# Rotary embedding in a decoder kernel: the sine products and sums of the rotation move from GpSimd to VectorE

## The reference

```
def apply_rope(t, freqs):
    rot = freqs.shape[-1]                       # 32 of the 64 features of a head
    t1, tp = (t[..., :rot], t[..., rot:])
    rh = jnp.concatenate([-t1[..., d2:], t1[..., :d2]], axis=-1)
    t1 = t1 * jnp.cos(freqs) + rh * jnp.sin(freqs)
    return jnp.concatenate([t1, tp], axis=-1)
...
q = q * DH ** (-0.5); q = apply_rope(q, pe_q); k = apply_rope(k, pe_k)
sim = jnp.einsum('bhid,bhjd->bhij', q, k)       # 8 heads of 64
a = jax.nn.softmax(sim, axis=-1)                # self-attention: masked first
out = jnp.einsum('bhij,bhjd->bhid', a, v)
```

## Time and profile before

| | |
|---|---|
| median of 3 runs | 4260.31 us (4253.38 to 4267.61) |
| profiled execution | 4263.09 us, its span 4261.1 us |
| busy | PE 3944.9 us (93%), DVE 2716.7 (64%), ACT 2011.2 (47%), POOL 986.7 (23%) |
| mean granted TensorE clock | 0.976 of full speed |

### The profile page before, as it was taken

The page is one execution under the profiler, slowest core; times in us unless marked ns, Lnnn a source line. Parts: engine busy times, 40 slices in busy tenths (PEclk is TensorE's granted clock), DMA queues, the critical chain, the costliest instruction groups (busy, mean ns, idle before and its releaser), DMA issues. The chain is left out here.

```text
span 4261.1 us, 70671 instructions
## 1 busy us (share of the span) xinstructions
PE 3944.9 (93%) x23644; PEld 2415.2 (57%) x23644; DVE 2716.7 (64%) x7580; ACT 2011.2 (47%) x5804; POOL 986.7 (23%) x1068
## 2 busy tenths in 40 slices
PE   7898899999999999999988988999999999999998
PEld 4644445565655655666646444455555556555665
DVE  4576667777777645764445776677777776456644
ACT  2633445555555534663226234456555555346632
POOL 2144423333222200000020443232333221000000
PEclk9899999999999999999988999999999999999999
DMA  2000000000000010010010000000000000100000
GB/s 91 6 17 1 1 23 17 23 17 23 17 23 2 25 57 21 14 53 9 8 54 5 17 1 1 23 17 23 17 23 17 23 2 25 71 7 34 33 9 10
DMA packets 15849, 91.84 MB, mean 22 GB/s; under 512 B 2176, under 2 KB 8064, under 8 KB 12032
## 3 DMA queue, kind: packets, MB, share of 16 engines
q1 hardware_dynamic: 15488, 87.27, 5.7%
HBM read 86.22 MB, written 1.05 MB: 20 GB/s over the span
## 5 line engine op out<-in xcount | busy, mean ns | idle before, releaser
L606 PE MATMUL ps_O<-wide,V 128*64 128x256 f32 (+4 forms) x5152 | 597.1, 395 | 1.9 <-ACT wide L634 1.8
L559 PE MATMUL ps_S<-KT,QT 64*128 64x154 f32 (+7 forms) x1936 | 383.4, 463 | 59.1 <-POOL QT L1614 25.4
L652 POOL COPY RX<-recips 128x256 f32<-128x256 f32 (+2 forms) x356 | 156.5, 440 | 1195.7 <-DVE recips L730 1184.8
L741 DVE TENSOR_TENSOR QT<-ps_O,RS 128x512 f32<-128x512 f32 x212 | 146.6, 692 | 413.9 <-PE ps_O L606 410.8
L687 ACT ACTIVATE EX<-NB,neg 128x154 f32<-128x154 f32 (+3 forms) x640 | 349.8, 551 | 103.7 <-DVE neg L715 103.7
L606 PEld LDWEIGHTS ps_O<-wide,V 128*64 128x64 f32 (+4 forms) x5152 | 266.9, 128 | 195.6 <-issue 112.0
L636 DVE COPY wide<-ps_P 128x512 f32<-128x512 f32 (+4 forms) x484 | 311.0, 645 | 80.8 <-PE ps_P L588 79.3
L429 POOL TENSOR_TENSOR small<-small 128x4 f32<-128x4 f32 x112 | 113.6, 1014 | 1042.8 <-DVE small L414 879.2
L634 ACT ACTIVATE wide<-ps_P 128x512 f32<-128x512 f32 (+4 forms) x488 | 274.9, 564 | 149.2 <-PE ps_P L588 149.1
L559 PE MATMUL ps_T<-KT,QT 64*128 64x154 f32 (+5 forms) x968 | 325.8, 439 | 17.1 <-ACT EX L687 9.0
L559 PE MATMUL ps_OUT<-KT,QT 64*128 64x154 f32 (+5 forms) x968 | 335.8, 442 | 0.9 <-ACT EX L687 0.4
(11 more groups left out here) (379 smaller groups left out, 8404.2 us busy)
## 6 DMA issues: line engine op xcount, KB each, us to landing
weights<-in_w_dram SPq DMA_DIRECT2D x10, 1664.0 KB, 6.8
weights<-in_w_dram SPq DMA_DIRECT2D x2, 6148.0 KB, 17.4
weights<-in_w5next_dram SPq DMA_DIRECT2D x6, 1664.0 KB, 6.8
weights<-in_w_dram SPq DMA_DIRECT2D x2, 4200.0 KB, 13.0
weights<-in_reltab_dram SPq DMA_DIRECT2D x2, 4096.0 KB, 13.6
weights<-in_w_dram SPq DMA_DIRECT2D x8, 640.0 KB, 3.9
weights<-in_w_dram SPq DMA_DIRECT2D x5, 832.0 KB, 4.4
weights<-in_w_dram SPq DMA_DIRECT2D x2, 2050.0 KB, 8.0
```

Of the source, the lines that this page charges most:

```text
L559: ins = pe.matmul(S4[k][:, a * N:(a + 1) * N], QT[strip, c, qts[a] * P:(qts[a] + 1) * P], self.keys(c)[strip, 0:N], start=True, stop=True)
L606: ins = pe.matmul(O1[self.slot * j:self.slot * (j + 1), q0 * P:(q0 + self.nq) * P], self.value(c * self.hpc + j, kc), self.probs(rd, j)[:, ...
L652: pool.tensor_copy(RX[:, q0 * P:(q0 + self.nq) * P].rearrange("p (n s) -> p n s", s=self.slot), of.unsqueeze(2).broadcast_to([P, self.nq * ...
L741: dve.tensor_tensor(self.out_chunk(c), O1[:, :], RS[:, c % 2, :], ALU.mult).then_inc(r.av_sb, 1)
```

## The change

DVE does the whole rotation: every product by the sines and every sum. POOL keeps the powers and the spreads, and issues both powers at the start of the step. The sum on DVE waits for the cosine product and the sine product of its own rope. The semaphores and their counts stay as they were; `rotated` is now raised by DVE.

```
@@ rope @@
-            if sin is not None:
-                dve.wait_ge(r.evac_dve, 2 * j + 1)
-                dve.tensor_tensor(part, part, sin, ALU.mult).then_inc(r.sum_step, 1)
+            dve.wait_ge(r.evac_dve, 2 * j + 1)
+            dve.tensor_tensor(part, part, sin, ALU.mult).then_inc(r.sum_step, 1)
+            dve.wait_ge(r.evac_dve, 2 * j + 2)
+            dve.wait_ge(r.sum_step, j + 1)
+            dve.tensor_tensor(dst, dst, part, ALU.add).then_inc(r.rotated, 1)
@@ Attention.pool @@
-            def pool(self, pool, r, late=None):
-                for i in range(1, self.rounds + 1):
-                    for j in self.late.get(i - 1, ()):
-                        if j != "X":
-                            late(pool, j)
-                    self.spread(pool, r, i - 1)
+            def pool(self, pool, r):
+                for rd in range(self.rounds):
+                    self.spread(pool, r, rd)
@@ L1Attention @@
             def turning(self, j):
                 return (self.part(j), 0.125 if self.order[j][0] == "q" else None, self.before(j), j,
-                        self.sines(j) if self.cross or j < 2 else None)
+                        self.sines(j))
-            def rotate(self, pool, j):
-                r, d, part = self.r, self.dest(j), self.part(j)
-                pool.wait_ge(r.evac_dve, 2 * j + 2)
-                if not self.cross and j >= 2:
-                    pool.tensor_tensor(part, part, self.sines(j), ALU.mult).then_inc(r.sum_step, 1)
-                pool.wait_ge(r.sum_step, j + 1)
-                pool.tensor_tensor(d, d, part, ALU.add).then_inc(r.rotated, 1)
             def pool(self, pool):
                 self.fresh(pool)
-                self.rotate(pool, 0)
-                self.rotate(pool, 1)
-                self.prev.pool_tail(pool)
-                if self.prev.tail_parts == 1:
-                    self.nxt.pool_head(pool)
-                self.rotate(pool, 2)
-                self.rotate(pool, 3)
-                if self.prev.tail_parts > 1:
-                    self.nxt.pool_head(pool)
-                self.att.pool(pool, self.r, self.rotate)
+                self.pool_beside(pool)
+                self.att.pool(pool, self.r)
```

## The result

| | before | after |
|---|---|---|
| median | 4258.98 us (4 runs, 4253.38 to 4267.61) | 4428.28 us (4 runs, 4420.55 to 4435.48) |
| profiled execution, its span | 4263.09 us, 4261.1 us | 4420.55 us, 4419.0 us |
| mean granted clock | 0.976 | 0.958 |
| 14 self steps, mean and all | 65.42, 915.9 us | 71.61, 1002.5 us |
| the first self step of each pass | 72.76, 72.75 us | 74.21, 75.82 us |

The ratio is 1.0386 [1.0370, 1.0401]: slower, as forecast. The median is 3 us above the top of the range (4325 to 4425; forecast 4384); the ratio times the 4260.3 us that the forecast started from is 4425, its edge. A step's length is taken from the first front projection to PE's first matmul of the next step. The two spans differ by 157.9 us: 86.6 in the 14 self steps, 4.5 in the two first ones, 64.1 in cross, 2.6 elsewhere.

What follows compares the result with a forecast made beforehand. PE, 93% busy, was taken as the bound, waiting for DVE at step fronts and late ropes. Self steps 61, cross steps 48 and clock 15 sum to +124 us: about 4384 us, range 4325 to 4425.

Steps and rivals of the forecast that it cites:

- self front: Self step up to the first row maximum: DVE's added rotation work moves it and PE's second scores by +3.25 us.
- self, late rope 5: Late product of rope 5: PE waits for the bank DVE empties, 0.52 us of slack against 1.32, losing 0.80 us.
- self, next bank: Self step after rope 5: DVE has room, 1.84 us idle ahead of rope 7's product, so nothing more is lost.
- the clock in self: Scores after PE's 3.1 us pause: TensorE's clock falls with weight 0.75, costing 1.4 us, 15 us over 14 steps.
- first self steps: First self step of each pass: POOL's power comes 1.15 us sooner, leaving at most 2.3 us added in each.
- cross step without clock: Cross step: sums on DVE delay maxima and the last exponentials of round 2, adding 3.0 us a step.
- 16 cross steps, clock included: All cross steps: 16 x 3.0 = 48 us, with no fall of the clock taken at pauses near 1.2 us.
- The price of a dependent sum: Each new DVE sum: 0.71 us for 512 columns, 0.34 for the 154-column keys; possible 0.61 to 0.85 for 512.
- The faster rival: PE's first scores: dropping its 25.4 us wait for POOL's sums and L438's collision gives some 4220 us; chance 0.05.
- The rule on mutual blocking: Skill's rule that two-SBUF-input DVE instructions and POOL block each other; some 11 us over 16 cross steps, left out.
- Partly hidden: Front shift is real but the rest, above all in cross, overlaps: +65 us, about 4325 us; chance 0.14.
- No change: DVE's room, 1.84 us idle against 1.32 more, takes in all the added work: 4260 us; chance 0.03.

Runs made afterwards that it cites:

- x1: Changed kernel with idle matmuls, read by nobody, filling PE's new pauses in self and cross steps; 4390.24 us, 1.0297 of before.
- x2: Changed kernel with the wait for the cosine product moved from the sum to the sine product, leaving the sum one wait; 4429.89 us.
- x3: Changed kernel with ropes 4 to 7 rotated by POOL again, as before the change; 4384.94 us, 1.0291 of before.
- x6: Kernel before with only the sums of ropes 0 and 1 moved to DVE; 4280.66 us, 1.0047 of before.
- x7: Kernel before without L438, its factor 1/128 applied behind the root inside L442 instead; 4252.81 us, 0.9977 of before.
- x5: Kernel before with two more 128x512 DVE products, read by nobody, ahead of round 0's maxima in each step; 4384.42 us.
- x9: Changed kernel with two more 128x512 DVE products, read by nobody, ahead of round 0's maxima; 4454.56 us.
- x10: Kernel before without L438, squares put behind round 0's maxima and POOL's head power behind its rotations 2 and 3; 4254.91 us, 0.9990 of before.

## Why the prediction was right, and where its sizes were off

The mechanism is the one forecast: DVE's row maxima come late, PE's pause ahead of the second scores grows from 0.59 us to 3.23 (forecast 3.1), and neither what POOL gives back nor DVE's idle time elsewhere covers it. The terms, by the two spans:

| term | forecast | measured |
|---|---|---|
| self front | +3.25 | +3.44 |
| self, late rope 5 | +0.80 | +0.93 |
| self, next bank | 0 | +0.36 (4.73 less the two above) |
| 14 self steps without clock | 56.7 us | 66 (14 x 4.73; filled: 981.9 - 915.9 = 66.0) |
| the clock in self | 15 us | 20.6 (x1) |
| first self steps | at most 4.6 us | 4.5 |
| cross step without clock | +3.0 | +3.7 (42.00 in x1 against 38.28) |
| 16 cross steps, clock included | 48 us | 64.1 |
| elsewhere | 0 | 2.6 |
| sum | 124 us | 157.8 |

- **The price of a dependent sum** was the step that failed most often. I took 0.71 us from a successor with one wait in front of it. This sum has two, and starts 0.11 instead of 0.03 us after its producer: 0.80, and 0.42 instead of 0.34 for the keys. x2 shows that the second wait makes the difference. It explains most of the front of self (ropes 2 and 3 take 2.77 us more, where two sums at 0.71 gave 2.64; the rest is rope 2's start, 0.66 later instead of 0.61), the late rope (0.80 + 0.09 = 0.89) and the cross step (four of each kind, 4 x 0.09 + 4 x 0.08 = 0.68 on 3.0 gives 3.68). Over 16 cross and 14 self steps that is 11 and some 4 us. The forecast's upper bound, 0.85, held it.
- **A second bank was missed.** I followed PE to its wait at rope 5 and took DVE to have room after it. The transposes at 1090.20 wait 0.17 us again, and the step is another 0.36 us longer than the two priced waits: 14 x 0.36 = 5 us. The rows place it here: from the late product to the scores behind the transposes it takes 1.86 us instead of 1.49. In x3, where POOL rotates the late ropes, the transposes come 0.97 us behind the product again.
- **The clock** fell behind 13 of 14 pauses of 3.23 us, where I had given it 0.75, and it cost 1.5 us each time, where I had 1.4. In cross I took none. It fell in all 16 steps and cost 0.45 each, 7 us: in 11 after or within the second of two pauses of 1.54 and 1.37 us, in 5 as soon as the first of them ended. The kernel before already had it in 2 of 16, with no pause over 0.97 us. The filled kernel shows both sizes by itself.
- **The faster rival** had POOL's slow sums decide. x6 tests the larger part of it alone (0.97 of the 1.59 us in a cross step) and comes out 0.5% slower. The forecast had put that wait into both kinds of step, and it stands in cross steps only. There PE's wait for the bank that DVE empties stands right behind it and grew from 0.53 to 1.12 us. And L438's 0.95 us, which the forecast gave back in full, is worth 0.16 us a self step and 0.44 a cross step when it goes alone (x7): the stretch saved ran into POOL's next sum or into PE's projection. In the changed kernel, where POOL no longer sums, no collision is left to meet: L440 takes 0.17 (above). So the forecast was right to count it there and would have been wrong to count it as a gain for itself.
- **The rule on mutual blocking** was set aside for the short product, and the sum went without it. For the change itself that was right: no product or sum is slowed, as the durations of the changed kernel show (ns, min/median/max). That holds beside POOL's power too: in the cross step above it ran from 763.10 for 1.01 us, and the 154-column product and sum that started at 763.39 and 763.80 took 0.31 and 0.32 us.

```profile
L364 DVE TENSOR_TENSOR NB<-NB,sinq x64: 674/681/691, 718.5 to 3721.7; 128x512 f32<-128x512 f32 x64
...
L367 DVE TENSOR_TENSOR QT<-QT,NB x64: 691/692/694, 719.3 to 3722.5; 128x512 f32<-128x512 f32 x64
```

  Had POOL kept rotations beside the new work of DVE, those instructions that started within one of POOL's could have cost 2.5 times as much (1.73 against 0.68, x5).
- **Partly hidden** (4325, chance 0.14): nothing was hidden in cross; a step is 3.7 us longer without the clock. **No change**: the change itself refutes it, and by x9 DVE has no room left in either kind of step of the changed kernel, where two products more cost 1.2 us.

Most of what was said of the trace came out so: sums at 0.69 and 0.32 us, a self step of 70.17 with the clock high and up to 72.25 with it low (69.5 to 71 said), DVE busy 175 us more (about 190 said). The cross step of 42.4 lies above the 41.2 that was said. For the 11.4 us by which the medians differ beyond the spans no run shows the cause. After, the mean clock was 0.958 in the execution of 4420.55 us and 0.952 in one of 4430.32, which fits a fall of the clock that comes out differently from run to run.

## What to carry to other kernels

Before moving elementwise work to the faster engine, ask which engine's result ends the next wait, and what stands in order ahead of it there: here 0.8 us a sum went one for one into the row maxima, though POOL needs 1.27 us for the same sum. Price a chain of dependent instructions by a row with the same number of waits in front of it, and follow the queue past the first wait that grows. A stall seen at one instruction is worth its duration only if what stands behind it doesn't meet the same obstacle, so test it alone before counting on it. And compare steps at the same granted clock before reading a few tenths of a us: here a fall of the clock in some of the steps was as large as the effect (x6, x7, x10).

## What the runs showed of the hardware

- A 128x512 product on DVE with two SBUF inputs takes 0.68 us alone. One that starts while a POOL sum or product of the same size runs takes 1.73; one that starts 0.2 to 0.3 us ahead of the sum keeps 0.68 to 0.76, and POOL's sum takes 1.59 instead of 1.27 (x5, x9). One over 154 columns that started 0.24 us into a POOL sum ended 0.19 us after it, 1.21 us instead of 0.31 (x10). Beside POOL's power over 128x4 (1.01 us) the same instruction keeps its 0.31 (after, at 763.39). DVE's row maxima, which read one of their two inputs from PSUM, kept their 0.68 to 0.70 us in x5.
- A DVE instruction that waits for its predecessor starts 0.03 to 0.04 us after that one's end with one wait and 0.11 after it with two, where an independent one starts 0.07 us before the end (0.61 after the start of a 0.68 us product). The Trainium skill (VectorE: DVE Perf Modes, The DRAIN you can't avoid) says of a chain of copies that a semaphore costs nothing extra. Here it cost 0.12 us with one wait (0.73 from start to start in x2, against 0.61) and 0.19 with two (0.80).
- The clock of TensorE fell to 1.2 GHz in all 16 cross steps of the changed kernel, where no pause was over 1.6 us, and once stayed at 2.4 behind a pause of 3.23 us. With no pause over 1.12 us it fell in 8 of 16 (x6), with none over 0.97 in 2 of 16 (before).
